# Phases that share buffers: the next phase's first weights and tokens are loaded in the last step of the phase before

## The chip, the cores and the metric

The kernel runs on one core of a Trainium2 chip. The time is the device time of one execution in microseconds, taken as the median of several executions. The engines of the core are TensorE (PE, with PEld for its weight loads), VectorE (DVE), ScalarE (ACT), GpSimd (POOL) and SyncE (SP), which here issues nearly all DMAs. Each engine works through its own list in order and meets the others only at semaphores. SBUF is the on-chip memory that DMAs fill.

## What is computed

A residual chain of four stages on x of shape (4, 1024, 512) in float32, in the order A, F, B, F, each of them x + stage(layernorm(x)) or the like:

```python
# mixer (A: 16 heads, state 64; B: 64 heads, state 128)
proj = x @ in_proj_w                       # z | x,B,C | dt
xBC = silu(causal_conv4(proj[..., xBC]))
y   = state_space_scan(xBC, softplus(dt + dt_bias), A_log) + D * x
out = rms_norm(y, silu(z)) @ out_proj_w
# F: a layer over tokens, with a message from the last token of each of 4 rows
x1  = layer_norm(x) ; h = x1[:, -1] @ agg_w + agg_b
for _ in range(4):                         # the recurrence, 4 columns wide
    h = h + gelu(layer_norm(h) @ d1_w + d1_b) @ d2_w + d2_b
msg = h @ bc_w + bc_b
o   = x1 + sigmoid(x1 @ gate_w + gate_b) * msg
```

## The kernel before

`build` runs four phases one after the other: `mixer_phase` for A, `ffn_phase`, `mixer_phase` for B, `ffn_phase`. Between phases x goes through DRAM tensors (`x_mid`). Each phase is a `nc.Block`: every engine has its own list, and at the end of a block all engines meet. A phase allocates its own SBUF buffers inside an ExitStack and gives them back at the end, so nothing of the next phase can be loaded before the block is over. Mixer A alone has its first buffers (`x_in`, `w_in`) allocated and loaded earlier, in `build_constants`, through the dictionary `early`.

A mixer works in NSUP = 16 supertiles of 256 tokens. `schedule` writes out TensorE's order; the projections of the next supertile are laced between the work of this one. The last supertile has no next one. SP's part is `step(i, m, prev, nxt)`: load the tokens of supertile m, store the second half of prev, load residual tiles, store the first half of i. `zza` and `zzb` are the last two products that read `w_in`; `gate_silu` is the last reader of `z_raw`; `silus` is the last reader of `cv`, and `halo` of `pre`. A mixer's prologue (before its first supertile) needs tokens, then the part of `w_in` from column 1024 on (`xbc_loaded`, L120), then the rest (`z_loaded`, L124).

An F phase first does the recurrence on 4 token rows, then 8 groups of 512 tokens. SP issues at its start, in this order: the last tokens (L1480), `agg_w`, `x_in` of group 0, `d1_w` (4 MB), `gate_w`, `d2_w` (4 MB), `x_in` of group 1, `bc_w`, two rows, and two residual groups. Then it goes through the groups: `store(n)` (L1478) waits for the group to be done and stores 1 MB, and `load_res(n + 2)` (L1474) waits for that store to have landed and loads 1 MB of residual.

The head of the recurrence, by engine:

- DVE: normalise the last tokens twice (L1723 to L1727, with a small power on POOL each time), `statistics(0)` (L1736, four reductions on `x_in` of group 0), two small operations that give `t_ready` (L1794), `aggregate(0)`, then the steps. In step 0 it does `statistics(1)`, which waits for `x_in` of group 1, and only after it the copy of `hid_rows` (L1817).
- PE: transpose the last tokens (L1563), `row_product(agg_w)` (L1550), `to_columns` (L1557), and then the steps. In step 0 only, `prepare(0, t)` for four tiles (L1510, transposes of the normalised group 0) stands between the mean (L1573) and the variance (L1582). L1590 is the d1 product, L1597 and L1605 follow `hid_rows` and the gelu. Pieces of the logits of groups 0 and 1 (L1521) are laid beside the steps.
- POOL: the two powers for the last tokens (L1895), then `in_scale(0)` (L1874 to L1877), which ACT's normalisation of group 0 (L1635) waits for.

Of the kernel before, what the change touches and what calls it, by code (L numbers as in the profile page):

```python
# [5 lines left out]
F32 = mybir.dt.float32  # L6
F32R = mybir.dt.float32r
BF16 = mybir.dt.bfloat16
# [3 lines left out]
P = 128  # L12
# [86 lines left out]

def load_vectors(eng, dst, w, H, loaded):  # L100
# [26 lines left out]
def build_constants(nc, ctx, ffn_w, mixers, weights, first_mixer_buffers):  # L127
# [35 lines left out]
    early = c["early"] = first_mixer_buffers()  # L163
    c["masked_bf"] = early["masked_bf"]
    with nc.Block() as block:
        @block.sync
        def _(sp):
            w = weights[mixers[0].tag]
            load_in(sp, early["x_in"], early["w_in"], early["xs_src"], w, early["x_loaded"], early["xbc_loaded"])
            load_z(sp, early["w_in"], w, early["z_loaded"])  # L170
# [59 lines left out]
def mixer_phase(nc, sig, before, cfg, c, early, later, psum, x_src, x_dst, w):  # L230
# [20 lines left out]
    with ctx:  # L251
# [3 lines left out]
        w_in = early["w_in"] if early else sb("w_in", [P, KD, cfg.proj])  # L255
# [6 lines left out]
        x_in = early["x_in"] if early else sb("x_in", [P, 2, DM])  # L262
# [4 lines left out]
        xn = sb("xn", [P, 2, DM])  # L267
        xnT = sb("xnT", [P, KD, SUP])
        pre = sb("pre", [P, NB, HALO + SUP])
        cv = sb("cv", [P, NB, SUP])  # L270
        xs = sb("xs", [P, KE, SUP])
        bcs = sb("bcs", [P, 2, SUP])
        z_raw = sb("z_raw", [P, KE, SUP])
# [232 lines left out]
        with nc.Block() as block:  # L506

            @block.sync
            def _(sp):
                for s in stored:  # L510
                    sp.sem_inc(s, STORED)
                if not early:
                    load_in(sp, x_in, w_in, xs_src, w, x_loaded, xbc_loaded)
                    load_z(sp, w_in, w, z_loaded)
# [23 lines left out]

                load_x(1)
# [14 lines left out]
                step(NSUP - 2, None, NSUP - 3, NSUP - 1)  # L554
                step(NSUP - 1, None, NSUP - 2, None)
# [808 lines left out]
def ffn_phase(nc, sig, before, tag, c, psum, x_src, x_dst, w):  # L1364
# [30 lines left out]
    with ctx:  # L1395
# [3 lines left out]
        d1_w, d2_w = sb("d1_w", [P, KD, HID]), sb("d2_w", [P, KH, DM])  # L1399
        agg_w, bc_w, gate_w = (sb(k, [P, KD, DM]) for k in ("agg_w", "bc_w", "gate_w"))  # L1400
# [3 lines left out]
        x_in, x_res0 = [sb(f"x_in{k}", [P, NT, DM]) for k in range(2)], sb("x_res", [P, NT, DM])  # L1404
# [16 lines left out]
        hid_rows, delta_rows = sb("hid_rows", [P, 512]), sb("delta_rows", [P, DM])  # L1421
# [41 lines left out]
        with nc.Block() as block:  # L1463
            @block.sync
            def _(sp):
# [16 lines left out]
                sp.dma_start(agg_w[:], w["agg_w"].rearrange("(k p) n -> p k n", p=P)).then_inc(w_agg, 16)  # L1482
                load_x(0)
# [501 lines left out]
```

## Time and profile before

| | |
|---|---|
| median of 3 executions | 3011.1 us (3009.7 to 3011.82) |
| the profiled execution | 3011.85 us, of which the span from first to last instruction is 3010.1 |
| mean granted TensorE clock in it | 0.967 |
| PE busy | 2792.6 us (93%) |
| DVE, ACT, POOL busy | 2018.7, 1248.8, 953.3 us |
| phases in the span, by SP's first DMA of each | A 0 to 1143, F 1143 to 1393, B 1393 to 2761, F 2761 to 3010 |

The page of the profile cuts the span into 40 slices of 75 us. TensorE is busy for nine tenths or more of nearly all slices; those that fall lower are the first, those around the three changes of phase, and the last. In the same slices the DMA engines move most of their bytes. A timeline row gives the start and the length in microseconds, the engine, the line, the operation, output and inputs, and how many instructions were merged into the row; the bracket says how long the engine sat idle before it and what ended that. DVE is the next busiest engine.

### The profile page before, as it was taken

What the parts mean: (1) busy time and instruction counts of PE and PEld (TensorE: products, weight loads), DVE (VectorE), ACT (ScalarE), POOL (GpSimd) and SP (SyncE); (2) the same over time, 40 slices, a digit from 0 to 9 for tenths busy, and PEclk for the clock granted to TensorE, in tenths of its full rate; (3) what the DMA queues carried; (4) which work ended last, traced back from release to release, by engine and by line L of the source; (5) the groups of instructions that cost most, each with busy time, mean ns of one, the idle gap of its engine ahead of it and who ended that gap; (6) DMA issues with size and microseconds to landing.
All of it is one profiled execution on the core that took longest, in us unless ns stands there. A gap on an engine that the chain in (4) does not pass through costs nothing. (4 is left out here: it accounts for less than half of the span.)

```text
span 3010.1 us, 54346 instructions
## 1 busy us (share of the span) xinstructions
PE 2792.6 (93%) x19824; PEld 1848.6 (61%) x19824; DVE 2018.7 (67%) x3697; ACT 1248.8 (41%) x2098; POOL 953.3 (32%) x618
## 2 busy tenths in 40 slices
PE   6999999999999996995899999999999999996896
PEld 5677666666667753454666666666666666663443
DVE  4656666656666662377777777777777777774267
ACT  3344443344434431341454444544445544442241
POOL 2322223222332230242333333333333333332134
PEclk9999999999999997997999999999999999997898
DMA  4000000000000006144000000000000000003433
GB/s 126 15 29 21 21 21 21 28 28 21 21 23 26 14 19 234 42 149 185 11 23 21 21 21 17 17 21 21 17 14 17 21 21 21 14 13 126 143 108 131
DMA packets 80674, 140.16 MB, mean 47 GB/s; under 512 B 18121, under 2 KB 18633, under 8 KB 79569
## 3 DMA queue, kind: packets, MB, share of 16 engines
q1 hardware_dynamic: 70448, 126.44, 12.2%
q10 hardware_dynamic: 10144, 12.64, 1.3%
q8 instruction: 51, 0.84, 0.1%
q14 instruction: 31, 0.25, 0.0%
HBM read 104.98 MB, written 33.55 MB: 46 GB/s over the span
## 5 line engine op out<-in xcount | busy, mean ns | idle before, releaser
L565 PE MATMUL work<-b_xnT,b_w_in 128*128 128x256 f32 x2304 | 548.3, 388 | 4.0 <-DVE b_parts L1077 3.9
L565 PE MATMUL work<-a_xnT,a_w_in 128*128 128x256 f32 x2176 | 501.6, 386 | 6.0 <-DVE a_parts L1077 4.7
L565 PEld LDWEIGHTS work<-b_xnT,b_w_in 128*128 128x128 f32 x2304 | 425.2, 191 | 87.3 <-issue 20.0
L565 PEld LDWEIGHTS work<-a_xnT,a_w_in 128*128 128x128 f32 x2176 | 409.4, 192 | 78.1 <-issue 18.3
L1117 DVE TENSOR_TENSOR b_decay<-b_decay,b_gt 128x1024 f32<-128x1024 f32 x256 | 354.3, 1421 | 28.4 <-ACT b_decay L841 24.4
L841 ACT ACTIVATE b_decay<-seg 128x1024 f32<-128x1024 f32 x256 | 251.3, 1021 | 174.8 <-PE seg L691 174.0
L1327 POOL TENSOR_TENSOR a_y<-a_y,a_skip 128x1024 f32<-128x1024 f32 x32 | 103.4, 3230 | 513.9 <-DVE a_y L1106 513.9
L1292 POOL TENSOR_TENSOR b_rhs<-b_l_side,of_head 128x1024 fp32r<-128x1024 f32 x32 | 82.0, 2563 | 578.8 <-DVE b_l_side L1086 578.8
L996 DVE SCALAR_TENSOR_TENSOR b_cv<-b_pre,b_conv_w,b_cv 128x256 f32<-128x256 f32 x480 | 222.5, 492 | 46.0 <-ACT b_cv L787 38.1
L672 PE MATMUL work<-b_w_out,b_yz 128*128 128x512 f32 x512 | 228.5, 599 | 8.3 <-DVE b_y L1106 8.3
L996 DVE SCALAR_TENSOR_TENSOR a_cv<-a_pre,a_conv_w,a_cv 128x256 f32<-128x256 f32 x432 | 189.7, 482 | 65.6 <-ACT a_cv L787 59.9
L672 PE MATMUL work<-a_w_out,a_yz 128*128 128x512 f32 x512 | 229.4, 601 | 3.5 <-DVE a_y L1106 3.4
L672 PEld LDWEIGHTS work<-b_w_out,b_yz 128*128 128x128 f32 x512 | 95.3, 191 | 118.0 <-issue 108.3
L672 PEld LDWEIGHTS work<-a_w_out,a_yz 128*128 128x128 f32 x512 | 95.7, 192 | 113.7 <-issue 108.8
L1117 DVE TENSOR_TENSOR a_decay<-a_decay,a_gt 128x1024 f32<-128x1024 f32 x64 | 151.1, 2383 | 11.5 <-ACT a_decay L841 11.0
L793 ACT COPY a_z_raw<-work 128x256 f32<-128x256 f32 (+1 forms) x96 | 42.2, 440 | 272.1 <-PE work L565 272.1
L1327 POOL TENSOR_TENSOR b_y<-b_y,b_skip 128x1024 f32<-128x1024 f32 x32 | 95.8, 2992 | 185.4 <-DVE b_y L1106 185.4
L705 PE MATMUL y<-b_decay,b_xdt 128*32 128x128 f32 x4096 | 139.8, 276 | 0.0
L705 PEld LDWEIGHTS y<-b_decay,b_xdt 128*32 128x32 f32 x4096 | 104.0, 110 | 52.3 <-issue 39.4
L1521 PE MATMUL y<-f_x1T,f_gate_w 128*128 128x512 f32 x256 | 130.1, 640 | 1.5 <-ACT f_x1T L1646 1.5
L786 ACT COPY b_pre<-work 128x256 f32<-128x256 f32 x160 | 59.8, 374 | 154.5 <-PE work L565 154.5
L1521 PE MATMUL y<-f_d_w,f_gate_w 128*128 128x512 f32 x256 | 111.5, 592 | 0.0
(311 smaller groups left out, 4617.2 us busy)
## 6 DMA issues: line engine op xcount, KB each, us to landing
f_d_w<-in_L_ffn_d_w SPq DMA_DIRECT2D x4, 4096.0 KB, 24.4
f_x_in<-x_mid ACTq DMA_DIRECT2D x12, 1024.0 KB, 6.1
a_x_in<-in_L_attn_a_x SPq DMA_DIRECT2D x16, 512.0 KB, 3.7
a_x_res<-in_L_attn_a_x SPq DMA_DIRECT2D x32, 256.0 KB, 2.6
x_mid<-a_x_res SPq DMA_DIRECT2D x32, 256.0 KB, 2.0
f_x_res<-x_mid SPq DMA_DIRECT2D x8, 1024.0 KB, 5.6
f_bc_w<-x_mid SPq DMA_DIRECT2D x8, 1024.0 KB, 5.5
b_x_in<-x_mid SPq DMA_DIRECT2D x16, 512.0 KB, 3.6
```

The costliest lines, as they stand in the source:

```text
L565: mm = nc.tensor.matmul(dst, w_in[:, k, col:col + m], xnT[:, k, :], start=(k == 0), stop=(k == KD - 1))
L672: mm = nc.tensor.matmul(bank[:, :], yz[:, k, :], w_out[:, k, :], start=(k == 0), stop=(k == KE - 1))
L705: mm = nc.tensor.matmul(ybank[32 * q:32 * q + 32, slot * P:(slot + 1) * P], xdt[:, j, 4 * slot + q, 16 * odd:16 * odd + 32], decay[:, slot ...
L786: nc.scalar.copy(pre[0:m, b, HALO:], bank[0:m, 0:SUP])
L793: nc.scalar.copy(z_raw[:, got[0]:got[-1] + 1, :], sec.bank(name)[:, 0:len(got) * SUP].rearrange("p (b t) -> p b t", t=SUP)).then_inc(z_rea ...
L841: nc.scalar.activation(decay[:, slot_buffer(j, s)].rearrange("p h l -> p (h l)"), seg[s % 2][:, :], ACT.Exp).then_inc(exp_done, 1)
L996: ins = nc.vector.scalar_tensor_tensor(out=cv[0:m, b, :], in0=pre[0:m, b, t:t + SUP], scalar=conv_w[0:m, b, t:t + 1], in1=cv[0:m, b, :], o ...
L1117: nc.vector.tensor_tensor(d, d, gt[:, j].unsqueeze(1).to_broadcast([P, 8, P]), ALU.mult).then_inc(m_ready, 1)
L1292: nc.gpsimd.tensor_tensor(rhs[1][:], l_side[:, 1].unsqueeze(1).to_broadcast([P, 8, P]), c["of_head"][:].unsqueeze(2).to_broadcast([P, 8, P ...
L1327: nc.gpsimd.tensor_tensor(y1[:], y1[:], skip[:], ALU.add).then_inc(y1x_ready, 1)
L1521: mm = nc.tensor.matmul(ybank[:, (m % 2) * 512:(m % 2 + 1) * 512], gate_w[:, k, m * P:(m + 1) * P], x1T[n][:, k, :], start=(k == 0), stop= ...
```

## The change

SBUF buffers that a phase needs first are cut out of five arrays that live for the whole program (`arenas`): one each under `w`, `cv`, `pre`, `z` and `x`. A mixer's `w_in`, `cv`, `pre`, `z_raw`, `x_in` and `xn` lie there, and so do an F phase's `d1_w`, `agg_w`, `gate_w`, both `x_in` and two row buffers. The last reader of each part in one phase frees it for the next phase's load, which SP issues (`load_next_phase`) with waits on those readers:

- in a mixer, between `step(14)` and `step(15)`: `agg_w` and `gate_w` after the last silu and halo, `d1_w` after `zzb`, `x_in` of group 0 after the last `gate_silu`;
- in the first F phase, in SP's group loop after `store(5)` and `load_res(7)`: tokens, then both parts of `w_in` of mixer B (5.1 MB in all).

These loads no longer stand at the phase starts. In the F phase, group 0's `statistics`, `aggregate`, `in_scale` and `prepare` are put ahead of the normalisation of the last tokens on DVE, POOL and PE. No operation on data is added or removed.

```diff
+def mixer_inputs(arena, cfg):
+    return cut(arena["x"], 0, 2, DM), cut(arena["w"], 0, KD, cfg.proj)
+def ffn_inputs(arena):
+    return {"d1": cut(arena["w"], 0, KD, 2048), "agg": cut(arena["cv"], 0, KD, DM), "gate": cut(arena["pre"], 0, KD, DM),
+            "x_in": [cut(arena["z"], 0, 4, DM), cut(arena["x"], 0, 4, DM)],
...
@@ mixer_phase, SP
-                if not early:
-                    load_in(sp, x_in, w_in, xs_src, w, x_loaded, xbc_loaded)
-                    load_z(sp, w_in, w, z_loaded)
...
+                def load_next_phase():
+                    to, fw = ffn_inputs(arena), c["ffn_w"]
+                    sp.wait_ge(silu_done, FREE + 2 * NSUP)
+                    sp.wait_ge(halo_done, FREE + NSUP)
+                    sp.dma_start(to["agg"], ...).then_inc(before("w_agg"), 16)
+                    sp.dma_start(to["gate"], ...).then_inc(before("w_gate"), 16)
+                    sp.wait_ge(work_full, last().full("zzb"))
+                    sp.dma_start(to["d1"], ...).then_inc(before("w_d1"), 16)
+                    sp.wait_ge(zs_done, NSUP)
+                    for t in stored:
+                        sp.wait_ge(t, STORED + 16 * 2)
+                    sp.dma_start(to["x_in"][0], by_group(x_dst)[0]).then_inc(before("x_loaded0"), 16)
...
                 step(NSUP - 2, None, NSUP - 3, NSUP - 1)
+                load_next_phase()
                 step(NSUP - 1, None, NSUP - 2, None)
@@ ffn_phase, SP
-                sp.dma_start(agg_w[:], ...).then_inc(w_agg, 16)
-                load_x(0)
-                sp.dma_start(d1_w[:], ...).then_inc(w_d1, 16)
-                sp.dma_start(gate_w[:], ...).then_inc(w_gate, 16)
                 sp.dma_start(d2_w[:], ...).then_inc(w_d2, 16)
                 load_x(1)
...
+                def load_next_phase():
+                    cfg, signals, mw = following
+                    to_x, to_w = mixer_inputs(arena, cfg)
+                    sp.wait_ge(x1_ready, NT * GROUPS)
+                    sp.wait_ge(o_full, NT * 5)
+                    sp.wait_ge(stored[0], 16)
+                    load_in(sp, to_x, to_w, by_supertile(x_dst), mw, signals("x_loaded"), signals("xbc_loaded"))
+                    load_z(sp, to_w, mw, signals("z_loaded"))
                 for n in range(GROUPS):
                     store(n)
                     if n + 2 < GROUPS:
                         load_res(n + 2)
+                    if n == 5 and following:
+                        load_next_phase()
@@ ffn_phase, PE
+                for t in range(NT):
+                    prepare(0, t)
                 pe.wait_ge(rows_ready, 1)
...
                     if step == 0:
-                        for t in range(NT):
-                            prepare(0, t)
                         pe.wait_ge(w_gate, 16)
@@ ffn_phase, DVE
+                link(statistics(0))
+                aggregate(0)
                 dve.wait_ge(last_loaded, 16)
                 normalise_last(0, LN_EPS)
                 normalise_last(1, EPS)
-                link(statistics(0))
...
                 nc.vector.tensor_tensor(t4, t4, over_b(in_beta), ALU.add).then_inc(t_ready, 1)
-                aggregate(0)
@@ ffn_phase, POOL
                 link(nc.gpsimd.memset(root[:], -0.5))
+                in_scale(0)
                 for k in range(2):
                     pool.wait_ge(rows_var, k + 1)
                     nc.gpsimd.tensor_tensor(l_r[:], l_v[:], root[0:BATCH, 0:1], ALU.pow).then_inc(rows_r, 1)
-                in_scale(0)
```

## Rows read from the trace of the kernel before

**Rows 1.** Page, part 1: busy time and share of the span of each engine.
```profile
PE 2792.6 (93%) x19824; PEld 1848.6 (61%) x19824; DVE 2018.7 (67%) x3697; ACT 1248.8 (41%) x2098; POOL 953.3 (32%) x618
```

**Rows 2.** Timeline, first F head, DVE: start, length, instruction [idle before <-releaser].
```profile
1143.86 0.11 DVE L1785 TENSOR_REDUCE f_batch_of<-ident 128x4 f32<-128x16 f32 x1
1144.77 0.68 DVE L1723 BATCH_NORM_STATS2 f_l_stats<-f_last 4x6 f32<-4x512 f32 x1 [0.80 <-DMA f_last<-x_mid]
...
1151.68 2.47 DVE L1736 BATCH_NORM_STATS2 f_stats<-f_x_in 128x6 f32<-128x512 f32 x4 [2.29 <-DMA f_x_in<-x_mid]
...
1182.03 2.48 DVE L1736 BATCH_NORM_STATS2 f_stats<-f_x_in 128x6 f32<-128x512 f32 x4 [10.90 <-DMA f_x_in<-x_mid]
1184.41 0.68 DVE L1817 COPY f_hid_rows<-seg 128x512 f32<-128x512 f32 x1
```

**Rows 3.** Timeline, the same stretch, PE, POOL and ACT.
```profile
1149.45 1.86 PE L1563 MATMUL seg<-ident,f_last 4*128 4x4 f32 x8 [9.73 <-DVE f_last L1727]
...
1154.63 1.93 PE L1550 MATMUL seg<-f_agg_w,f_tt 128*32 128x512 f32 x8 [3.32 <-DVE f_tt L1795]
1154.96 0.25 POOL L1874 TENSOR_SCALAR f_neg_mean<-f_mv 128x4 f32<-128x4 f32 x1 [6.14 <-DVE f_mv L1745]
...
1156.99 2.92 ACT L1635 ACTIVATE f_x<-f_x_in,f_shift,f_r_in 128x512 f32<-128x512 f32 x4 [12.57 <-POOL f_shift L1877]
...
1161.23 3.80 PE L1510 MATMUL work<-ident,f_x 128*128 128x128 f32 x16
...
1165.80 2.05 PE L1521 MATMUL y<-f_x1T,f_gate_w 128*128 128x512 f32 x2 [0.77 <-ACT f_x1T L1646]
...
1173.60 3.64 PE L1590 MATMUL seg<-f_d_w,f_tt 128*32 128x512 f32 x32
```

**Rows 4.** Timeline, the second F head: the same product and the same copy.
```profile
2791.27 3.64 PE L1590 MATMUL seg<-f_d_w,f_tt 128*32 128x512 f32 x32
...
2801.77 0.67 DVE L1817 COPY f_hid_rows<-seg 128x512 f32<-128x512 f32 x1
```

**Rows 5.** DMA view of 1140 to 1200: GB/s in 40 slices of 1.5 us, loads, issue-to-landing.
```profile
GB/s 8 167 5 150 375 363 347 441 431 437 437 426 410 388 391 386 392 386 385 388 392 380 386 386 384 388 386 385 392 384 382 71 3 0 0 0 0 0 30 190
...
f_agg_w<-in_L_ffn_agg_w SPq DMA_DIRECT2D x1, 1024.0 KB, 5.3
f_gate_w<-in_L_ffn_gate_w SPq DMA_DIRECT2D x1, 1024.0 KB, 19.4
```

**Rows 6.** Windows view (stretch, then busy us by engine, granted clock, DMA share, GB/s).
```profile
1184.00:1187.00 3.00, 1.85 (x6) 1.25 (x6) 1.58 (x7) 0.26 (x1) 0.00 (x0) 0.50 0.93 343
```

**Rows 7.** Timeline, DVE: end of step 0, then copy and end of step 1.
```profile
1195.09 0.17 DVE L1830 TENSOR_TENSOR f_th<-f_th,seg 128x16 f32<-128x16 f32 x1 [1.90 <-PE seg L1557]
...
1203.87 0.69 DVE L1817 COPY f_hid_rows<-seg 128x512 f32<-128x512 f32 x1 [1.38 <-PE seg L1590]
...
1212.86 0.17 DVE L1830 TENSOR_TENSOR f_th<-f_th,seg 128x16 f32<-128x16 f32 x1 [1.91 <-PE seg L1557]
```

**Rows 8.** Timeline, end of the first F phase and head of mixer B.
```profile
1372.97 0.37 SPq L1474 DMA_DIRECT2D f_bc_w<-x_mid  x1
...
1388.54 0.38 SPq L1478 DMA_DIRECT2D x_mid<-f_bc_w  x1
...
1393.43 0.38 SPq L119 DMA_DIRECT2D b_x_in<-x_mid  x1
...
1404.05 3.67 PE L594 MATMUL work<-b_w_in,b_xnT 128*128 128x64 f32 x16 [1.81 <-DMA b_w_in<-in_L_attn_b_in_proj_w]
```

**Rows 9.** Timeline, head of mixer A, whose inputs were there: the first DMA and the same product.
```profile
16.22 0.37 SPq L515 DMA_DIRECT2D a_w_out<-in_L_attn_a_out_proj_w  x1
...
23.29 3.57 PE L594 MATMUL work<-a_w_in,a_xnT 128*128 128x16 f32 x16 [0.77 <-ACT a_xnT L771]
```

**Rows 10.** Timeline, mixer A's last supertile: the gate and the last residual.
```profile
1094.95 1.91 ACT L812 ACTIVATE a_zs<-a_z_raw 128x2048 f32<-128x2048 f32 x1
...
1139.85 0.75 DVE L1162 SCALAR_TENSOR_TENSOR a_x_res<-work,a_rr,a_x_res 128x512 f32<-128x512 f32 x1 [5.70 <-PE work L672]
```

More of the change, by code:

```diff
@@ L124, in load_z, with by_supertile, by_group, build_constants @@
     sp.dma_start(w_in[:, :, 0:E], w["in_proj"].rearrange("(t p) n -> p t n", p=P)[:, :, 0:E]).then_inc(z_loaded, 16)
[L127 removed]
+def by_supertile(x):
+    return x.rearrange("(s j p) d -> s p j d", p=P, j=2)
+def by_group(x):
+    return x.rearrange("(g t p) d -> g p t d", p=P, t=4)
+def build_constants(nc, ctx, ffn_w, mixers, weights, arena, mixer_signals, x_src, first_mixer_buffers):
     def sb(name, shape, dt=F32):
@@ L227, in build_constants, with mixer_phase @@
     return c
-def mixer_phase(nc, sig, before, cfg, c, early, later, psum, x_src, x_dst, w):
+def mixer_phase(nc, sig, before, cfg, c, arena, later, psum, x_src, x_dst, w):
     H, HP, N, NS = cfg.H, cfg.HP, cfg.N, cfg.slots
@@ L537, in step @@
                         load_res(nxt, 0)
+                def load_next_phase():
+                    to, fw = ffn_inputs(arena), c["ffn_w"]
+                    sp.wait_ge(silu_done, FREE + 2 * NSUP)
+                    sp.wait_ge(halo_done, FREE + NSUP)
+                    sp.dma_start(to["agg"], fw["agg_w"].rearrange("(k p) n -> p k n", p=P)).then_inc(before("w_agg"), 16)
+                    sp.dma_start(to["gate"], fw["gate_w"].rearrange("(k p) n -> p k n", p=P)).then_inc(before("w_gate"), 16)
+                    sp.wait_ge(work_full, last().full("zzb"))
+                    sp.dma_start(to["d1"], fw["d1_w"].rearrange("(k p) n -> p k n", p=P)).then_inc(before("w_d1"), 16)
+                    sp.wait_ge(zs_done, NSUP)
+                    for t in stored:
+                        sp.wait_ge(t, STORED + 16 * 2)
+                    sp.dma_start(to["x_in"][0], by_group(x_dst)[0]).then_inc(before("x_loaded0"), 16)
                 load_x(1)
@@ L1397, in sb @@
             return ctx.enter_context(nc.sbuf_tensor(f"{tag}_{name}", shape, dt))
-        d1_w, d2_w = sb("d1_w", [P, KD, HID]), sb("d2_w", [P, KH, DM])
-        agg_w, bc_w, gate_w = (sb(k, [P, KD, DM]) for k in ("agg_w", "bc_w", "gate_w"))
+        loaded = ffn_inputs(arena)
+        d1_w, agg_w, gate_w, x_in = loaded["d1"], loaded["agg"], loaded["gate"], loaded["x_in"]
+        d2_w, bc_w = sb("d2_w", [P, KH, DM]), sb("bc_w", [P, KD, DM])
         in_gamma, in_beta, pn_gamma, pn_beta = (c["ffn"][k] for k in ("in_gamma", "in_beta", "pn_gamma", "pn_beta"))
@@ L1403, in ffn_phase @@
         gamma_row, beta_row = sb("out_gamma_row", [P, DM]), sb("out_beta_row", [P, DM])
-        x_in, x_res0 = [sb(f"x_in{k}", [P, NT, DM]) for k in range(2)], sb("x_res", [P, NT, DM])
+        x_res0 = sb("x_res", [P, NT, DM])
         x1 = sb("x1", [P, NT, DM])
@@ L1420, in ffn_phase @@
         hid = sb("hid", [P, KH, COLS])
-        hid_rows, delta_rows = sb("hid_rows", [P, 512]), sb("delta_rows", [P, DM])
+        hid_rows, delta_rows = loaded["rows"]
         batch_of = sb("batch_of", [P, BATCH])
```

52 lines of the change are left out of this document (28 added, 24 removed).

## Prediction

> **What bounds the kernel now.** I read the page first: TensorE is busy for 93% of the span [rows 1], so a change that only moves loads can win only where TensorE stands still. These places are the phase changes, so I then read the timeline of the first 60 us of each F phase and of the head of mixer B, engine by engine, and the DMA view of the same stretch.
>
> In the F head the reader is to see a serial chain across DVE, PE and POOL. It starts when the last tokens land, at 1144.77 [rows 2], and their transposes start on PE at 1149.45, the end of 9.73 us without a matmul there [rows 3]. DVE then waits 2.29 us for the tokens of group 0 and reduces them for 2.47 [rows 2], although nothing in the recurrence needs that. PE goes on at 1154.63, 0.48 after the reductions end. Later 16 transposes of group 0 stand in the chain, from 1161.23 to the next product at 1165.80 [rows 3]. The largest stall comes last. PE ends the d1 product at 1173.60 + 3.64 = 1177.24 [rows 3], but DVE has the statistics of group 1 ahead of the copy that must follow, and these wait 10.90 us for a DMA; the copy starts at 1184.41 [rows 2]. The transfers behind it are 11 MB in one queue, moved at about 385 GB/s until 1187 [rows 5].
>
> At the head of mixer B the engines have met at about 1393.4, and the first product that reads weights starts at 1404.05, ended by the DMA of those weights [rows 8]. Mixer A, whose inputs were there, shows the same stretch without that wait [rows 9].
>
> **The change part by part.**
>
> *Loads moved ahead of the F phases.* Tokens of group 0, `agg_w`, `gate_w` and `d1_w` (7.3 MB) are issued in the mixer's last supertile. `agg_w` and `gate_w` wait for the last silu, `d1_w` for the last use of `w_in`, which is just before the gate's silu at 1094.95 [rows 10], the tokens for that silu. At 385 GB/s [rows 5] the 5.2 MB of `d1_w` and tokens take 14 us, so they are there by about 1110, well ahead of the phase's start at 1143. On SP the second half store of supertile 14 and the last residual load are queued behind them. They would land a few us late, but the last residual is added at 1139.85 [rows 10], some 25 us later. Cost: nothing, covered by that margin; without the cover it would be up to the 14 us.
>
> *What the stall becomes.* At the F start SP now has `d2_w` and then the tokens of group 1 ahead: 5.2 MB, 13.6 us at 385 GB/s and some 2.6 of fixed time (`agg_w`, 1 MB, first in the queue, took 5.3 us, of which 2.7 are its bytes [rows 5]). ACT's load of group 2 (1 MB) runs beside it: 2.7 more. That is 1162 to 1163; the statistics must start by 1172.8 to be off the path. So the copy follows the product directly, as it does in step 1. The gain is 1184.41 - 1177.24 - 0.07 = 7.1 us. In the second F phase it is 2801.77 - (2791.27 + 3.64) - 0.07 = 6.8 us [rows 4]. Together 13.9. What is late next is PE's product itself, since DVE is idle before it.
>
> *The norm of group 0 ahead.* DVE's last set-up operation ends at 1143.97 [rows 2]. The reductions now start there and end 2.47 later, at 1146.4; the aggregates take at most 0.81 (from the end of the reductions to POOL's start at 1154.96, two small operations included [rows 2, 3]); I take 0.5. POOL's `in_scale` and the hand-over to ACT take 1156.99 - 1154.96 = 2.03 [rows 3], so ACT normalises from 1149.0 to 1151.9. The chain of the last tokens, 1149.45 - 1144.77 = 4.7 us [rows 2, 3], starts at 1146.9 instead, and its first power waits for POOL to end `in_scale`, 0.9 more: ready at 1152.5. But on PE the 16 transposes stand ahead of it. They take 3.80 without waits [rows 3], begin when ACT has a first tile (1149.7), and the third and fourth wait until ACT, which does its four tiles first, copies the first two out. They end between 1153.5 and 1155.7; I take 1154.8. The transposes of the last tokens (1.86 [rows 3]) end at 1156.7, and with 0.6 for DVE, PE's next product starts at 1157.3 instead of 1154.63: 2.7 later, between 1.4 and 3.6. Against that 1165.80 - 1161.23 = 4.6 us go in step 0 [rows 3]. Net 1.9 us gained in each F phase (1.0 to 3.2), 3.8 in both.
>
> *The clock.* After the stall the granted clock is 0.50, the lower of the two levels, for 1184 to 1187 [rows 6]. Step 0 takes 1195.09 - 1184.41 = 10.68 us from the copy to its end, step 1 takes 1212.86 - 1203.87 = 8.99 [rows 2, 7]. Without the idle time I expect the second: 1.7 us in each, 3.4 together. Before the d1 product TensorE is also at the lower level, and whether it rises sooner with matmuls started sooner the trace can't say. Bounds: 1.5 us lost to 4 us gained in each F phase; I take nothing.
>
> *The end of the first F phase.* The weights and tokens of mixer B (5.4 MB) enter SP's queue right behind the residual load issued at 1372.97 [rows 8], and two stores of 1 MB come behind them; the last, issued at 1388.54, is what ends the phase, and B's first DMA follows it at 1393.43 [rows 8]. From 1372.97 these are 8.5 MB: 22.1 us at 385 GB/s plus 2.6, so 1397.7. At the fastest slice, 441 GB/s [rows 5], it is 1394.9. The last store must have landed before 1393.43; I put it at 1392.8, so the phase ends 2.1 to 4.9 us later. I take 4.0. The queue does work in order: `gate_w`, 1 MB behind 4 MB of `d1_w`, took 19.4 us to land [rows 5].
>
> Against this speaks one rule. The Trainium skill, page "DMA: Bandwidth & Descriptors", section "Two DMAs through the same engine are not ordered", says that nothing orders transfers across the 16 engines and that a later one may be done first. If the store went past the weights in this way the 4.0 would be 0 and the sum 4 us lower. The same page, section "Specifications", gives an HBM limit of about 358 GB/s per core; the trace shows 385 to 441 here, and the measurement decides. By the page's figure the delay would be some 1.7 us more, as an estimate.
>
> *The head of mixer B.* It loses the wait for tokens and for weights. Before: 1404.05 - 1393.43 = 10.62 us from SP's first DMA to the first product [rows 8]. Mixer A, with its inputs there: 23.29 - 16.22 = 7.07 [rows 9]. Gain 3.5. The later `z` part was not waited for before. With the late end of the phase this is a net loss of 0.5 us (between a gain of 3.5 and a loss of 1.4).
>
> *The start of mixer A, and the end of the kernel*, keep their order and their loads: nothing.
>
> **The sum.** 13.9 + 3.8 + 3.4 - 0.5 = 20.6 us less. The profiled execution took 3011.85 us, so 2991.2 for one like it. The median of the runs is 0.75 lower, 3011.1, so 2990.5.
>
> **The rivals.**
>
> 1. *More from the clock.* TensorE reaches the full clock sooner in both F heads, and no other dip follows. Up to 4 us in each: 2982. For it: the matmuls start 1149.7 instead of being spread from 1149.45 on with gaps. Against it: the products just before the stall move only 1.9 us, and the transposes that kept PE busy there are gone. The case in which the store passes the weights (2986.5) lies between.
> 2. *Less.* The store waits the full 4.9, the clock gives nothing after the stall and PE's order costs its upper end: 3.4 + 1.8 + 0.9, so 2996.6, and with 1.5 lost to the clock in each phase, 2999.6.
> 3. *The tokens of group 1 are still late*, since `d2_w` (4 MB) still stands ahead of them. Then only 3.8 - 0.5 = 3.3 us come: 3007.8. Against it: it takes 10 us of delay beyond the sum of bytes. That is also the case of a change which doesn't do what it says, when the last step's waits hold the loads back.
> 4. *Slower, by the clock.* Without the 16 transposes in step 0 the stretch before the d1 product is thin, and TensorE might stay at the lower level through the recurrence. A half step costs 1.7 us more there; eight half steps less the one already paid make 7 x 1.7 = 12 us in each phase, 24 in both, and the 3.4 aren't gained. 3011.1 - 17.2 + 24 = 3018. It decides from the point where the clock is not up by the start of step 1. Against it: the logits' products, 512 columns wide, stay where they were.
>
> **How the numbers follow.** Forecast, 2984 to 2997: 0.57. Rival 1: 0.17. Rival 2: 0.15. Rival 3: 0.07. Rival 4: 0.04. The range of 2978 to 3001 takes in the forecast and the first two rivals. A measurement of this kernel can tell 0.2%, 6 us, from no change: faster by more 0.89, within it 0.07, slower 0.04.
>
> **What would show it.** In the changed profile: no DMA releaser ahead of DVE's second set of reductions, and the `hid_rows` copy 0.1 us after the d1 product; that copy 31.6 us behind DVE's last set-up operation instead of 1184.41 - 1143.86 = 40.6; PE's `agg_w` product 2.7 us farther from it; the step from copy to end at 9.0 us; the first F phase's last store landing near 1397 less what was gained before; 7.1 us from mixer B's first DMA to its first product. The prediction is wrong if the clock dips elsewhere in the recurrence, if the second reductions still wait for a DMA, or if the mixers' last supertiles grow.

## The result

The changed kernel takes 2984.9 us (median of four executions, 2983.7 to 2990.3) against 3010.4 for the kernel before on the same chip: ratio 0.9921, 95% interval 0.9905 to 0.9936. Two later timings gave 0.9921 (0.9904 to 0.9937) and 0.9927 (0.9913 to 0.9942); over all 13 executions of it the median is 2985.8 us. The forecast was 2990.5, or 0.9932.

The profiled execution is the longest of the first four, 2988.6 us in span, 21.5 less than before. The page's first part has the same work and less time:

```profile
span 2988.6 us, 54351 instructions
...
PE 2784.4 (93%) x19824; PEld 1846.6 (62%) x19824; DVE 2020.4 (68%) x3697; ACT 1249.0 (42%) x2098; POOL 955.8 (32%) x618
```

The F head, DVE in the timeline. These rows answer to [rows 2]. The reductions of group 0 start right behind the last set-up operation, and the second ones have no DMA ahead of them:

```profile
1143.80 0.11 DVE L1843 TENSOR_REDUCE f_batch_of<-ident 128x4 f32<-128x16 f32 x1
1143.94 2.47 DVE L1794 BATCH_NORM_STATS2 f_stats<-shared_z 128x6 f32<-128x512 f32 x4
...
1169.13 0.17 DVE L1871 TENSOR_TENSOR f_tt<-f_cen,pn_beta 128x16 f32<-128x16 f32 x1
1169.22 2.46 DVE L1794 BATCH_NORM_STATS2 f_stats<-shared_x 128x6 f32<-128x512 f32 x4
1176.40 0.69 DVE L1875 COPY shared_w<-seg 128x512 f32<-128x512 f32 x1 [4.71 <-PE seg L1648]
...
1185.85 0.17 DVE L1888 TENSOR_TENSOR f_th<-f_th,seg 128x16 f32<-128x16 f32 x1 [1.91 <-PE seg L1615]
```

PE in the same stretch, against [rows 3]:

```profile
1149.91 1.97 PE L1568 MATMUL work<-ident,f_x 128*128 128x128 f32 x8 [10.24 <-ACT f_x L1693]
1153.15 1.94 PE L1568 MATMUL work<-ident,f_x 128*128 128x128 f32 x8 [1.27 <-ACT f_x1T L1704]
1155.02 1.87 PE L1623 MATMUL seg<-ident,f_last 4*128 4x4 f32 x8
1157.36 1.94 PE L1608 MATMUL seg<-shared_cv,f_tt 128*32 128x512 f32 x8 [0.48 <-DVE f_tt L1854]
...
1167.39 5.37 PE L1579 MATMUL y<-f_x1T,shared_pre 128*128 128x512 f32 x6
1172.69 3.64 PE L1648 MATMUL seg<-shared_w,f_tt 128*32 128x512 f32 x32
```

The copy follows the d1 product by 0.07 us (1172.69 + 3.64 = 1176.33) instead of 7.2. But that product is preceded by six logits matmuls that take 5.37 us at the lower clock (0.50, 1.2 of 2.4 GHz), although DVE had its input ready at 1169.3 (the row of L1871). In this order TensorE itself is the bound from 1164 on: its timeline has no idle time from there to the copy.

The end of the first F phase and the head of mixer B, against [rows 8]. SP issues the last store, then B's first DMA; then the first product with B's weights:

```profile
1362.11 0.37 SPq L1524 DMA_DIRECT2D f_bc_w<-x_mid  x1
...
1377.69 0.38 SPq L1528 DMA_DIRECT2D x_mid<-f_bc_w  x1
1386.30 0.38 SPq L547 DMA_DIRECT2D b_w_out<-in_L_attn_b_out_proj_w  x1
```

```profile
1393.34 1.94 PE L642 MATMUL work<-shared_w,b_xnT 128*128 128x64 f32 x8 [0.77 <-ACT b_xnT L819]
```

Cut at such rows, every execution traced falls into stretches that can be compared. The table is worked out from the start times of five kinds of rows: DVE's last set-up operation (S), the first hid_rows copy, F's last store, B's first DMA, B's first weight product. "Step 2" runs from one `th` addition to the next, as in [rows 7]; where a time is given for step 0 alone (9.45 us and the like), it runs from the first copy to the first `th` addition. The code counts steps from 0, and where an expectation below says first, third or last half step it means steps 0, 2 and 3.

| kernel (us) | S of F1 | S to copy, F1 / F2 | step 2, F1 / F2 | F1: S to last store | store to B's DMA | to product | to S of F2 | F2: S to end |
|---|---|---|---|---|---|---|---|---|
| before | 1143.9 | 40.6 / 40.3 | 22.3 / 22.4 | 244.7 | 4.9 | 10.6 | 1357.5 | 248.6 |
| changed | 1143.8 | 32.6 / 31.9 | 21.4 / 21.5 | 233.9 | 8.6 | 7.0 | 1356.1 | 239.2 |
| e1 (changed) | 1143.1 | 32.5 / 32.0 | 21.4 / 21.5 | 233.7 | 8.7 | 7.0 | 1355.9 | 237.7 |
| e10 (changed) | 1143.0 | 32.5 / 32.0 | 21.4 / 21.5 | 233.7 | 8.6 | 7.0 | 1355.9 | 238.1 |
| e2 norm back | 1144.0 | 27.7 / 31.6 | 22.5 / 21.6 | 230.6 | 8.9 | 7.0 | 1355.8 | 237.6 |
| e9 norm back | 1142.7 | 27.7 / 31.8 | 22.5 / 21.6 | 230.4 | 8.7 | 7.0 | 1355.6 | 238.0 |
| e3 tokens first | 1144.5 | 30.1 / 33.5 | 21.2 / 22.3 | 238.0 | 4.9 | 10.4 | 1357.3 | 241.9 |
| e12 order only | 1138.4 | 40.0 / 39.2 | 21.6 / 21.2 | 241.5 | 4.9 | 10.5 | 1355.8 | 245.0 |
| e4 B at its start | 1138.0 | 32.7 / 32.4 | 21.4 / 21.7 | 233.7 | 4.9 | 10.7 | 1358.8 | 238.6 |
| e5 z last | 1140.7 | 32.7 / 32.5 | 19.8 / 21.4 | 232.3 | 6.1 | 7.0 | 1355.9 | 238.4 |
| e6 one more | 1137.8 | 32.7 / 32.5 | 18.0 / 18.0 | 230.5 | 8.7 | 7.0 | 1358.5 | 235.0 |
| e7 fill | 1142.5 | 30.7 / 30.6 | 22.7 / 22.7 | 233.2 | 8.7 | 7.0 | 1358.8 | 237.8 |
| e8 three edits | 1144.0 | 27.7 / 27.6 | 18.0 / 18.0 | 225.6 | 6.0 | 7.0 | 1358.9 | 230.2 |
| e11 best | 1144.8 | 27.6 / 27.7 | 18.0 / 18.0 | 225.1 | 5.3 | 7.0 | 1356.4 | 230.1 |

The account of the 21.5 us between the two profiled executions: mixer A 0.1, the first F phase 10.8, B's head 3.6 and B's body 1.4 less, the second F phase 9.4 less, and the last store 3.7 more, rounded each. (The second F phase is 237.7 and 238.1 us in the two other traces of the change, so its 9.4 is the low end.)

### The profile page after: what moved, and what is told of

Read it like the earlier page. It is cut to its first block and busy times, and to the rows that moved or that the text cites. A ratio compares the mean times of both kernels' runs of the same rounds, so it can differ in the third digit from the quotient of the medians.

```text
span 2988.6 us, 54351 instructions
## 1 busy us (share of the span) xinstructions
PE 2784.4 (93%) x19824; PEld 1846.6 (62%) x19824; DVE 2020.4 (68%) x3697; ACT 1249.0 (42%) x2098; POOL 955.8 (32%) x618
## 5 line engine op out<-in xcount | busy, mean ns | idle before, releaser
L613 PE MATMUL work<-b_xnT,shared_w 128*128 128x256 f32 x2304 | 548.6, 389 | 6.2 <-DVE b_parts L1125 6.1
L613 PE MATMUL work<-a_xnT,shared_w 128*128 128x256 f32 x2176 | 501.6, 386 | 6.1 <-DVE a_parts L1125 4.8
L613 PEld LDWEIGHTS work<-b_xnT,shared_w 128*128 128x128 f32 x2304 | 425.4, 191 | 89.4 <-issue 20.0
L613 PEld LDWEIGHTS work<-a_xnT,shared_w 128*128 128x128 f32 x2176 | 409.4, 192 | 78.2 <-issue 18.3
L841 ACT COPY shared_z<-work 128x256 f32<-128x256 f32 (+1 forms) x192 | 84.8, 442 | 414.3 <-PE work L613 414.3
L1044 DVE SCALAR_TENSOR_TENSOR shared_cv<-shared_pre,b_conv_w,shared_cv 128x256 f32<-128x256 f32 x480 | 222.4, 492 | 46.4 <-ACT shared_cv L835 38.6
L1044 DVE SCALAR_TENSOR_TENSOR shared_cv<-shared_pre,a_conv_w,shared_cv 128x256 f32<-128x256 f32 x432 | 189.7, 482 | 65.8 <-ACT shared_cv L835 60.1
L834 ACT COPY shared_pre<-work 128x256 f32<-128x256 f32 x304 | 113.5, 373 | 287.8 <-PE work L613 287.8
L1579 PE MATMUL y<-f_x1T,shared_pre 128*128 128x512 f32 x256 | 128.9, 636 | 0.0
L1382 POOL TENSOR_TENSOR b_xw<-b_xdt,b_e 128x512 f32<-128x512 f32 x64 | 106.0, 1675 | 0.0
```

Of the source, the lines that this page charges most:

```text
L613: mm = nc.tensor.matmul(dst, w_in[:, k, col:col + m], xnT[:, k, :], start=(k == 0), stop=(k == KD - 1))
L834: nc.scalar.copy(pre[0:m, b, HALO:], bank[0:m, 0:SUP])
L841: nc.scalar.copy(z_raw[:, got[0]:got[-1] + 1, :], sec.bank(name)[:, 0:len(got) * SUP].rearrange("p (b t) -> p b t", t=SUP)).then_inc(z_rea ...
L1044: ins = nc.vector.scalar_tensor_tensor(out=cv[0:m, b, :], in0=pre[0:m, b, t:t + SUP], scalar=conv_w[0:m, b, t:t + 1], in1=cv[0:m, b, :], o ...
L1382: ins = nc.gpsimd.tensor_tensor(xw4[:, :, odd, :], xdt[:, j, :, 32 * odd:32 * odd + HP], e4[:, :, odd:odd + 1].to_broadcast([P, H // 2, HP ...
L1579: mm = nc.tensor.matmul(ybank[:, (m % 2) * 512:(m % 2 + 1) * 512], gate_w[:, k, m * P:(m + 1) * P], x1T[n][:, k, :], start=(k == 0), stop= ...
```

## The experiments

**e1, the changed kernel again.** No edit.

> The changed kernel once more, unaltered, for a second trace. Its four executions lay between 2983.7 and 2990.3 us, and the one that was profiled was the longest. Theory: the work is the same in each, and the 6 us are the granted clock, which dips in the third half step of the recurrence (0.66 in 1210 to 1215, with the d1 product at 4.74 us instead of 3.64) in one execution and not, or shorter, in another. If so, a profile near 2984 shows that product at 3.6 and the third half step at 18 to 20 us, not 21.4, in one or both F phases. Rival: the difference lies elsewhere, in the mixers (a slice of lower clock there) or in the landing of a transfer; then the F heads are as they were, 32.6 us to the copy, 9.45, 17.8 and 21.4 for the steps, and the mixer phases differ.

Measured 2985.1 us (2984.0 to 2987.9), span 2986.2. The theory fell: step 2 takes 21.4 us in this execution too. Where executions differ with the same code is seen best at the end of mixer A, whose code none of the edits of e2 to e12 touches: it comes at 1137.8 in some and 1144 in others (table). The three traces of the change itself all have it at 1143 to 1144. The windows view of the changed kernel, then of e4 (columns: stretch, busy us of PE, PEld, DVE, ACT, POOL, granted clock, DMA share, GB/s):

```profile
1112.00:1118.00 6.00, 5.68 (x21) 2.60 (x14) 3.63 (x5) 1.55 (x4) 2.05 (x1) 0.50 0.19 45
```

```profile
1112.00:1118.00 6.00, 5.59 (x14) 2.69 (x15) 5.77 (x8) 0.41 (x2) 5.18 (x2) 1.00 0.02 8
```

TensorE has some 2.3 us of idle time in two gaps (0.6 and 1.7 us) between 1106 and 1112 in the last supertile of both; in one the granted clock then falls to the lower of its two levels, in the other it stays. That is worth 5 to 6 us at the end of mixer A and is not of the change: the kernel before falls too, and e12, which has its loads, does not.

**e2 and e9, the norm of group 0 back in its old place, loads moved.**

```
 PE:    - for t in range(NT): prepare(0, t)          (ahead of the last tokens)
        + for t in range(NT): prepare(0, t)          (in step 0, behind the mean)
 DVE:   - link(statistics(0)); aggregate(0)          (ahead of normalise_last)
        + link(statistics(0)) behind normalise_last; aggregate(0) behind t_ready
 POOL:  - in_scale(0) ahead of the two powers        + behind them
```

> The changed kernel with the norm of group 0 back in its old place (DVE, POOL and PE order as before), the moved loads kept. The parts add up if the recurrence's head is a chain of work alone: the stall of 7.1 us stays gone, so the first hid_rows copy comes 40.6 - 7.1 = 33.5 us after DVE's last set-up operation, against 32.6 with both parts. By the forecast's own term this kernel is 1.9 us slower per F phase than the change, 3.8 in all; by the trace of the change it is 0.9 per phase, 1.8 in all. Rival: with the tokens of group 0 long there, the old order costs nothing (DVE's 2.3 us of waiting for them is gone as well), and this kernel is as fast as the change or up to 3 us faster.

> The kernel of the run with the norm of group 0 back in its old place once more, beside the change on the same chip and in five rounds. Three of the four F phases traced with that order and with the moved loads had the clock up at about +19 us and the first hid_rows copy at 27.6 us; the fourth, and all twelve traced with the norm ahead, had it up at about +27 and the copy at 30.6 to 32.7. Theory: the order with the norm ahead is a loss by itself, 0.4 to 1.1 us per phase by TensorE's gaps and up to 5 where the clock comes sooner, so this kernel is 3 to 7 us faster than the change, and in one or both of its F phases the copy comes at 27.7. Rival: the sooner rise is chance and spread evenly over both orders; then the two kernels differ by less than 2 us.

> The changed kernel, unaltered, in five rounds, to compare with. Theory: 2983 to 2986 us, with the first hid_rows copy at +31.9 to +32.7 in both F phases as in all traces of it so far. Rival: the clock comes up at +19 in one of them too, and the copy is at +28.

e2: 2982.1 us, 0.9905 (0.9888 to 0.9922). e9: 2981.7, 0.9904 (0.9888 to 0.9919), beside e10, the change, with 2988.0, 0.9927 (0.9913 to 0.9942). Over all executions 2981.7 (8) against 2985.8 (13). The intervals overlap, so a pair alone would not decide, but both pairs and the traces point the same way: on top of the moved loads the new order, one half of the change, is a small loss. e2's theory fell and its rival holds; e9's theory holds (6.4 us faster, one copy at 27.7); e10 has its copies where they were expected and a median 2 us above its range. PE of e2 in the first F phase:

```profile
1152.38 1.94 PE L1608 MATMUL seg<-shared_cv,f_tt 128*32 128x512 f32 x8 [0.94 <-DVE f_tt L1853]
...
1165.20 2.82 PE L1579 MATMUL y<-f_x1T,shared_pre 128*128 128x512 f32 x6
1167.95 3.64 PE L1648 MATMUL seg<-shared_w,f_tt 128*32 128x512 f32 x32
```

and in the second:

```profile
2769.19 4.98 PE L1579 MATMUL y<-f_x1T,shared_pre 128*128 128x512 f32 x6
2774.11 3.64 PE L1648 MATMUL seg<-shared_w,f_tt 128*32 128x512 f32 x32
```

The same six matmuls take 2.82 us or 4.98. The windows view of e2, the same place of both phases:

```profile
1164.00:1170.00 6.00, 6.00 (x36) 2.67 (x38) 2.89 (x7) 0.69 (x1) 1.01 (x1) 1.00 0.80 302
2766.00:2772.00 6.00, 6.00 (x14) 3.42 (x15) 1.40 (x5) 0.00 (x0) 1.01 (x1) 0.50 0.82 314
```

The clock is up 18 to 20 us behind S in one phase and 26 to 28 behind it in the other, with the same work before it. With the loads moved and the old order the sooner rise came in six of eight heads traced (e2, e8, e9, e11), with the new order as it is in the change in none of twelve (changed, e1, e4, e5, e6, e10); e7, below, is a case of its own. Where it comes sooner the copy is 4.9 us sooner, and some 1.1 us of that go again in step 2 (22.5 for 21.4), so F1 is 3.3 us shorter (230.4 against 233.7). Where it doesn't, the orders differ by 0.2 to 0.4 us at the copy (e9 against e10, e2 against e1, second phases).

**e12, the order without the loads.** The mirror image of that edit in the kernel before.

> The kernel before with the norm of group 0 ahead of the recurrence on DVE, POOL and TensorE, and no load moved. DVE now waits for the tokens of group 0, which land 7.8 us behind its last set-up operation, before it touches the last tokens. Theory: the agg_w product and its copy come 5.2 + 7.7 us later than with the old order, at +23.3; the d1 product ends at about +40.3 (32.6 + 7.7), which is when the tokens of group 1 land and their statistics end (+40.5) anyway. So the stall swallows the delay and the time is that of the kernel before within 3 us: the order alone is worth nothing, neither way. Rival: the clock rises the later for it, the d1 product runs at the lower level, and each F phase is 3 to 5 us longer than before, 6 to 10 in all.

Measured 3001.7 us, 0.9978 (0.9964 to 0.9993). The prices of the parts were right, the conclusion was not: DVE waits 7.72 us for the tokens, the transposes follow late, the d1 product too, and the statistics of group 1 hardly delay the copy any more:

```profile
1146.26 2.47 DVE L1736 BATCH_NORM_STATS2 f_stats<-f_x_in 128x6 f32<-128x512 f32 x4 [7.72 <-DMA f_x_in<-x_mid]
...
1175.12 2.47 DVE L1736 BATCH_NORM_STATS2 f_stats<-f_x_in 128x6 f32<-128x512 f32 x4 [3.50 <-DMA f_x_in<-x_mid]
1178.38 0.69 DVE L1817 COPY f_hid_rows<-seg 128x512 f32<-128x512 f32 x1 [0.79 <-PE seg L1590]
```

The copy comes only 0.6 and 1.1 us sooner than before. But the idle time is now ahead of TensorE's work (17.94 us before its first transposes) instead of in its middle, and the clock, once up, stays up through the first two steps: step 0 takes 9.45 us in both phases against 10.7 and 10.95, and step 2 about 1 less. The rival was right that the clock rises later, 34 to 36 us behind S against 28 to 29 in the kernel before, and wrong on what that costs. By the table the F phases are 3.2 and 3.6 us shorter, 6.8 together; the ratio says 6.6, the medians 9. The order alone gains a little; it is on top of the moved loads that it loses.

**e3, two lines exchanged in the kernel before.**

```
+ load_x(1)
  sp.dma_start(d2_w[:], w["d2_w"]...)
- load_x(1)
```

> The kernel before with two lines exchanged in both F phases: the tokens of group 1 (1 MB) are issued ahead of d2_w (4 MB) instead of behind it. Nothing else is moved. The queue lands in order, so the tokens are there before the d1 product ends, and d2_w lands where the tokens did, at about 1184.3 by the time of the first F phase. The d2 product wants it 3.1 us after the copy (1179.5 - 1176.4 in the change), at 1180.4, and waits until 1184.4; it came at 1187.5. So the stall falls from 7.1 to about 4 us and the gain is 3.1 us per F phase, 6 in all: 3004 to 3006. Rival: the transfers run beside each other and d2_w is there in time, then the whole 7 us per phase go, 2996. If the stall were not from the landing order at all, nothing changes.

Measured 2997.1 us, 0.9958 (0.9944 to 0.9972): 12 us, half of the change's gain, from one exchange. By the table each F phase is 6.7 us shorter. The stall is gone and a shorter one on `d2_w` takes its place:

```profile
1182.83 5.34 PE L1605 MATMUL seg<-f_d_w,f_hid 128*32 128x512 f32 x32 [5.10 <-DMA f_d_w<-in_L_ffn_d_w]
```

```profile
2793.27 3.21 PE L1605 MATMUL seg<-f_d_w,f_hid 128*32 128x512 f32 x28 [1.55 <-DMA f_d_w<-in_L_ffn_d_w]
```

Both waits end 38.2 to 38.4 us behind S, where the tokens of group 1 landed before (1182.03 - 1143.86 = 38.2 [rows 2]): the queue lands in order. My expectation had this at 40.4, because I took the start of the copy for the landing of the tokens, which comes 2.4 us sooner, ahead of the reductions. In F1 the clock rose sooner, at about +21 (once in the four heads traced with this order and without the moved loads), and the wait on `d2_w` swallowed that.

**e4, mixer B's weights and tokens loaded at B's own start.**

```
-                    if n == 5 and following: load_next_phase()
+                if cfg.tag == "b":                      (first lines of the mixer's SP)
+                    load_in(...); load_z(...)
```

> The changed kernel with mixer B's weights and first tokens loaded at B's own start, as before the change; everything else as changed. Theory: the moved load delays the last store of the first F phase by 3.7 us (store to B's first DMA 8.6 us against 4.9) and saves 3.6 at B's head (7.0 against 10.6), so the two cancel and this kernel takes the same time as the change within 1 us. Rival: the load delays nothing and 3.5 us are lost here; or the delay is the larger part (the trace of the change has 1.4 us less in B's body as well), and the difference lies between 1 us faster and 2 us slower.

Measured 2986.8 us, 0.9926 (0.9910 to 0.9943). From the last store to the product it is 4.9 + 10.7 = 15.6 us, in the changed kernel 8.6 + 7.0 = 15.6: B's load in the first F phase gives at the head what it takes at the end. The theory holds by the trace; the medians (2986.8 beside e1's 2985.1) are too close to add to it. B's body is 2.9 us longer here, but so it is in e6 to e8, which keep the load; it isn't the load. These four have a dip of the clock some 16 us before B's end (e4: 0.54, 0.50 and 0.50 in the three stretches of 2 us from 2730 on), where the changed kernel has 1.00.

**e5, the z part of B's weights behind the last store.**

```
   sp.wait_ge(stored[0], 16); load_in(sp, to_x, to_w, ...)
-  load_z(sp, to_w, mw, signals("z_loaded"))
   for n in range(GROUPS): store(n) ...
+  load_z(...)
```

> The changed kernel with one load of mixer B moved: the z part of its input weights (the last 2 MB of the 5.4) is issued behind the last store of the first F phase instead of ahead of the last two stores. In the change the store has 8.61 us to B's first DMA; from the residual load at 1362.1 on there are 8.5 MB, 22 us at 385 GB/s, which is the delay. Without the z part there are 6.4 MB, 16.6 us, and the store is issued 15.6 us behind that load, so only its own bytes are left. Theory: store to B's first DMA falls back to 4.9 us, the first weight product keeps its 7.0, z arrives before it is used, and the kernel is 3.7 us faster than the change: about 2981.5. Rival: B's head is held by z instead, because its product comes a few us after the first one; then a DMA wait shows in B's first supertile and the gain is 0 to 2 us.

Measured 2984.5 us (2979.6 to 2987.3), 0.9922 (0.9904 to 0.9940): by the times alone, undecided. By its trace the store takes 6.1 us instead of 8.6, and the product still comes 7.0 behind B's first DMA, so z is in time. The gain is 2.5 us, not 3.7; z, issued 0.43 us behind the store, still costs it 1.2.

**e6, one logits product from the last step to the first.**

```
- PRODUCTS = [(1, 3, 2, 1, 2, 1), ..., (1, 3, 2, 1, 2, 1)]
+ PRODUCTS = [(1, 3, 2, 2, 2, 1), ..., (1, 3, 2, 1, 1, 1)]
```

> The changed kernel with one of the logits products moved from the last half step of the recurrence to the first (its row in the table of products gets 2 beside the hid transposes instead of 1; the last row 1 beside d2 instead of 2). It doesn't undo a part of the change: it tests what makes the third half step 21.4 us where the second has 17.8. In the trace ACT copies the fourth block of logits only after the 16th product, at 1204.5, then normalises group 2, and TensorE waits 0.69 and 1.30 us for these tokens, then the granted clock is 0.66 for 1210 to 1215. With one product more in the first step the 16th comes 1.75 us sooner. Theory: the two waits shrink from 2.0 us to about 0.3, the clock stays up, and the third half step takes 17.8 to 19; the first takes 0.95 more, the last 0.95 less. Gain 1.7 to 3.4 us per F phase, 3.5 to 7 in all: 2978 to 2981.5. Rival: the clock dips there anyway, since the stretch is thin for another reason; then 1.7 us per phase at most. Or ACT is not what holds the group: then nothing.

Measured 2980.7 us (2978.9 to 2982.8), 0.9911 (0.9895 to 0.9928). The change was not timed beside it, so the theory is judged by the trace. ACT in the changed kernel, then in e6. In the first it waits for the 16th product and only then normalises:

```profile
1204.59 0.69 ACT L1721 ACTIVATE f_gate<-y,gate_b 128x512 f32<-128x512 f32 x1 [7.51 <-PE y L1579]
1205.17 2.92 ACT L1693 ACTIVATE f_x<-shared_z,f_shift,f_r_in 128x512 f32<-128x512 f32 x4
```

```profile
1197.75 0.69 ACT L1721 ACTIVATE f_gate<-y,gate_b 128x512 f32<-128x512 f32 x1 [5.76 <-PE y L1579]
1198.34 2.92 ACT L1693 ACTIVATE f_x<-shared_z,f_shift,f_r_in 128x512 f32<-128x512 f32 x4
```

Of the waits of 0.69 and 1.30 us on PE one of 0.15 is left, the clock is 1.00 where it was 0.66, and step 2 takes 18.0 us in all six phases traced with this edit (e6, e8, e11). Step 0 has 0.86 more, step 3 0.76 less. The F phases are 3.2 and 3.1 us shorter than in e10: the theory holds. e5's first phase has the gaps and not the dip (19.8), so of the 3.4 us the gaps are about 1.8 and the clock the rest.

**e7, three logits products in TensorE's gaps ahead of the recurrence.**

```
+ one_ahead()            behind the transposes of the last tokens
+ one_ahead()            behind row_product(agg_w)
+ one_ahead()            behind to_columns(1)
- PRODUCTS = [(1, 3, 2, 1, 2, 1), ...      + PRODUCTS = [(0, 1, 2, 1, 2, 1), ...
```

> The changed kernel, with three of the four logits products that stand ahead of the d1 product in the first half step issued earlier, in the three gaps of TensorE before the recurrence (behind the transposes of the last tokens, behind the agg_w product and behind its transposes). Only the norm of group 0 ahead makes that possible. As many products stand ahead of the d1 product as before. Theory: from 20 us behind DVE's last set-up operation TensorE has no gap at all, so what counts is only its gaps before that (0.5, 0.5, 0.3 and 0.3 us from +12 to +20) and the moment at which the clock rises; the order of its work counts for nothing. The gaps filled, the first hid_rows copy comes 1.2 to 1.6 us sooner, at +31 to +31.5 instead of +32.5, and the kernel is 2.4 to 3.2 us faster than the change. Rival: the clock rises sooner with TensorE gapless, at +20 instead of +27; then the copy comes at +27 and the gain is 5 us per phase. Or the products delay the serial chain by their 1.8 us each and nothing is gained.

Measured 2984.8 us, 0.9920 (0.9903 to 0.9936), so nothing of the 2.4 to 3.2 us shows in the time. The copy is 1.8 and 1.4 us sooner than in e10, close to what the sum of the gaps said. The sum is not the whole of it, though, for the clock does come sooner, as the rival said, and does not stay. It is up from 18 to about 22 us behind S in both phases, falls behind an idle time of 0.48 us, and rises for good at about +28. PE in the first phase, then the windows view of it:

```profile
1162.78 0.95 PE L1642 MATMUL seg<-f_th,mean_w 128*128 128x4 f32 x8
1164.20 1.87 PE L1647 MATMUL seg<-f_sq,mean_w 128*128 128x4 f32 x8 [0.48 <-DVE f_sq L1872]
1165.93 2.05 PE L1580 MATMUL y<-f_x1T,shared_pre 128*128 128x512 f32 x2
1167.92 5.17 PE L1655 MATMUL seg<-shared_w,f_tt 128*32 128x512 f32 x32
```

```profile
1161.00:1163.00 2.00, 2.00 (x14) 1.50 (x13) 0.17 (x1) 0.00 (x0) 0.00 (x0) 1.00 1.05 410
1165.00:1167.00 2.00, 2.00 (x8) 1.41 (x7) 0.16 (x1) 0.00 (x0) 0.57 (x1) 0.50 0.90 335
```

The d1 product takes 5.17 us here instead of 3.64, as most of it falls at the lower level. Step 2 takes 22.7 us in both phases for 21.4, and F1 as a whole is 0.5 us shorter. e7's windows view in that step, against a dip of 5 us at 0.66 in the first phase of the changed kernel:

```profile
1204.00:1209.00 5.00, 3.70 (x17) 1.93 (x20) 2.89 (x7) 2.51 (x5) 1.01 (x1) 0.62 0.57 160
1209.00:1214.00 5.00, 5.00 (x33) 1.04 (x26) 0.00 (x0) 0.00 (x0) 0.00 (x0) 0.70 0.14 53
```

What is gained ahead of the gap in step 2 is partly given back in it. The dip itself is no longer than the one in the second phase of the changed kernel, which begins at 2811, earlier in the step, and costs less there (21.5). Why it comes where it does the runs do not tell.

**e8 and e11, the edits together.** e8 is norm back, z last and one more; e11 has the z part behind the waits for the last stores.

> Three edits at once, against the change: the old order of group 0's norm, the z part of B's weights behind the last store, and one logits product moved to the first half step. Their parts by what the runs have shown so far: 0.4 to 1.1 us per F phase from the order with the clock's rise where it was, up to 5 where it comes sooner; 3.7 us from the store; 1.7 to 3.4 per F phase from the third half step. Sum 8 to 13 us less than the change: 2972 to 2977. Rival: the parts overlap in the clock, so that one dip avoided brings another in the same phase, and less than 6 us are left.

> Loads moved, group 0's norm in its old place, one logits product moved to the first half step, and the z part of B's weights issued behind the waits for the last stores instead of ahead of them. With z ahead of these waits the store still took 6.07 us to B's first DMA, 1.2 more than the 4.9 without any load. Theory: z behind the waits gives 4.9, so 1.2 us less than the 2972.8 of the kernel with these three edits: about 2971.5, 13 less than the change. Rival: z then arrives late for B's first supertile, and 1 to 3 us come back there.

e8: 2972.8 us (2972.0 to 2973.5), 0.9882 (0.9866 to 0.9899). e11: 2970.2 us (2967.0 to 2970.7), 0.9865 (0.9849 to 0.9881), 18 less than the change timed beside it (e10; 16 less than the median of all its executions) and 40 less than the kernel before. The parts add, and with the gap of step 2 gone the sooner clock keeps its whole 4.9 us: e8's F phases are 4.9 and 4.7 shorter than e6's. SP of e11 at the end of the first F phase:

```profile
1369.91 0.38 SPq L1528 DMA_DIRECT2D x_mid<-f_bc_w  x1
1374.27 0.38 SPq L151 DMA_DIRECT2D shared_w<-in_L_attn_b_in_proj_w  x1
1375.18 0.38 SPq L547 DMA_DIRECT2D b_w_out<-in_L_attn_b_out_proj_w  x1
```

The store is through 4.4 us after its issue, and B's first DMA in the sense of the table comes at 5.3, the issue of z among it. So 0.8 us of the 1.2 came. z is not late: B's first product keeps its 7.0, and B's body is not longer (1356.4).

## Why the prediction held, and where it did not

*The stall behind the second reductions* (13.9 us): right, and shown from two sides: e3 removes it by the order in the queue alone, and e2 removes it by the loads alone. The tokens of group 1 were issued at 1143.93 and took 18.3 us, so they landed at 1162.2; the sum had said 1162 to 1163. DVE asked for them at 1169.2. The DMA view of 1140 to 1200:

```profile
shared_x<-x_mid SPq DMA_DIRECT2D x1, 1024.0 KB, 18.3
```

*The norm of group 0 ahead* (3.8): the times were nearly right and the credit wrong. The `agg_w` product was put at 1157.3 and came at 1157.36. But the step that failed is the comparison: I set this against 1154.63, a time that holds DVE's 2.29 us of waiting for the tokens of group 0, which the moved loads remove alone. In e2 the product comes at 1152.4. So the order costs the chain 5.2 us, not 2.7, against 4.6 saved in step 0. By this sum the loads were worth 2.4 us per phase more than I gave them and the order was worth -0.6; measured at the copy, with the clock rising at the same place, the order is worth -0.2 to -0.4. Of the 1.9 us net, 0.9 and 1.5 were there at the copy (40.6 to 32.6 and 40.3 to 31.9, less 7.1 and 6.8), because TensorE, not the chain, is the bound before the d1 product. I had followed the chain and not summed up TensorE's work at the lower clock.

*The clock after the stall* (3.4): right in kind, 1.2 and 1.5 us instead of 1.7 each. I had measured step 0 by step 1, 8.99 us; undisturbed it takes 9.45. Another 0.9 us came in each step 2, which the sum had left out.

*The clock before the d1 product* (nothing, -1.5 to 4): nothing, in this kernel. The gain of rival 1 exists, e2 has it in one phase, and the heads with the order of the change do not (none of twelve, against six of eight). It is not the order as such: e7 keeps the norm ahead, fills three gaps, and has the sooner rise in both heads, for 4 us. The Trainium skill, page "TensorE: Matmul & The Clock Gate", section "What's actually happening", says that the slow level is the default and activity releases it. The traces agree so far as they were read here: idle time comes before the falls, and e7's filled gaps bring a sooner rise. But e2's two phases show the release 8 us apart behind the same work, so that rule doesn't date it.

*The signs.* The copy was put 31.6 us behind S and came at 32.6 and 31.9; the last store was put near 1397 less the gain, and 1386.3 plus the 10.8 of the first F phase is 1397.1. One sign of being wrong was a clock that dips elsewhere in the recurrence. It does dip in step 2, but it did so before the change as well (kernel before, then changed):

```profile
1215.00:1220.00 5.00, 3.61 (x21) 2.97 (x22) 2.11 (x7) 3.77 (x7) 1.01 (x1) 0.69 0.19 50
```

```profile
1210.00:1215.00 5.00, 5.00 (x30) 1.02 (x32) 1.63 (x3) 0.51 (x1) 0.00 (x0) 0.66 0.53 195
```

*The end of the first F phase* (+4.0): 3.7. The queue works in order, and e5 and e11 show the cause by taking it away (6.1 and 5.3 for 8.6). That a later transfer might pass an earlier one, which would have taken the 4.0 away, did not happen. *The head of B* (-3.5): -3.6. *The loads in the last supertile* (nothing): S at 1143.80 against 1143.86.

The sum was 20.6 us and the profiled execution has 21.5 less. The agreement is in part luck: the norm gave 1.4 us less than forecast and the clock behind the stall 0.7 less, while step 2, which had no term, gave 1.8 more. The median moved by 25.5 in that timing and 23 to 24 in the two later ones. What is beyond the sum is probably the ends of the mixers, where an execution has 3 to 6 us more or less by its clock; but the three executions of the change that were traced all have the slow end of mixer A, so none shows the fast one and this is argued only. Rivals 2 to 4 did not come: none of the traces of the change has a DMA ahead of the second reductions, or a clock still low in step 1.

What stays open: what decides whether the clock rises at 19 or 27 us, and falls in a gap of 2 us or not. The same code does both. What in the work makes the sooner rise likely is open too; the gaps ahead of it, as e7 shows, are part of it.

## What to carry to other kernels

When one edit has two parts, price each on top of the other and not only against the kernel before: a wait that both would remove was credited to the wrong one here, and the half that lost went unseen. Where an engine is saturated at its lower clock, sum its work and its gaps; the order of a serial chain beside it says little. And before weights are moved across phases, look at the order within the queue: two lines exchanged gave half of the gain.

## What the hardware showed that I had not expected

- With the same instructions before it, the granted clock went up about 19 or about 27 us behind S; six of eight heads took the first with one order of the same work, none of twelve with the other. With the gaps of that other order filled (e7) it went up at about 18 in both heads and was down again 4 us later.
- Gaps of 0.69 and 1.30 us in TensorE's work are followed by a stretch at the lower level in some executions and not in others: 19.8 us for step 2 in e5 against 21.4; gaps of 0.6 and 1.7 us do the same at the end of mixer A, 6 us apart. In the second phase of the changed kernel the clock fell behind the first gap alone, so that four transposes took 1.12 us where they take 0.65:

```profile
2810.96 1.12 PE L1568 MATMUL work<-ident,f_x 128*128 128x128 f32 x4 [0.69 <-ACT f_x L1693]
```

- An SP instruction that issues a load can itself take long while transfers are queued. The issue of 1 MB of tokens behind 4 MB of weights took 4.49 us in the changed kernel; in the kernel before, behind 11 MB, it took 20.46 (the third row):

```profile
1143.47 0.41 SPq L1532 DMA_DIRECT2D f_d_w<-in_L_ffn_d_w  x1
1143.93 4.49 SPq L1517 DMA_DIRECT2D shared_x<-x_mid  x1
1148.42 20.46 SPq L1467 DMA_DIRECT2D f_x_in<-x_mid  x1
```
